# Later layers of a two-block transformer: the input product of the GELU layer in fp16 parts, four norms of a steady iteration on another engine, and a new order of stages around them

## The reference, cut to what matters

```python
x2 = _layernorm(x, g1, be1)
q = x2 @ wq.T ; k = x2 @ wk.T ; v = x2 @ wv.T        # elu + 1 on q and k
x = x + linear_attention(q, k, v)
x2 = _layernorm(x, g2, be2)                          # this is y below
h = gelu(x2 @ w1.T + b1, approximate=False)          # w1: 1024 x 256
x = x + (h @ w2.T + b2)
```

## Time and profile before

| | |
|---|---|
| median of 3 runs | 3226.55 us (3226.42 to 3232.63) |
| the profiled execution | 3230.64 us |
| its span in the trace | 3228.8 us |
| mean granted TensorE clock | 0.979 |
| PE busy | 2933.4 us, 91% |
| ACT busy | 2332.3 us, 72% |
| DVE busy | 1480.0 us, 46% |
| POOL busy | 214.9 us, 7% |

### The profile page before, as it was taken

How to read it: one execution, slowest core, us unless ns; L and a number is a source line. 1 busy time by engine, 2 the same in 40 slices (tenths; PEclk the granted TensorE clock), 3 DMA queues, 4 the chain that set the end, 5 groups by cost and what they waited for, 6 DMA issues and landing times. The chain is left out here.

```text
span 3228.8 us, 48001 instructions
## 1 busy us (share of the span) xinstructions
PE 2933.4 (91%) x18048; PEld 1173.8 (36%) x18048; DVE 1480.0 (46%) x3536; ACT 2332.3 (72%) x2586; POOL 214.9 (7%) x193
## 2 busy tenths in 40 slices
PE   2998998999999999999999998389999999999986
PEld 0221221222222222222222222256666666666654
DVE  6221220322441333232321311568888888866574
ACT  2999999999999999999999998224343334433332
POOL 0000000000000000000000000111111111111110
PEclk9999999999999999999999999699999999999998
DMA  3411111310210221111211110222122111111010
GB/s 115 141 40 36 61 37 35 102 37 33 91 39 30 88 62 42 63 35 54 71 42 35 38 41 24 64 71 60 53 71 73 59 58 58 46 53 53 26 46 21
DMA packets 125602, 177.70 MB, mean 55 GB/s; under 512 B 42248, under 2 KB 100616, under 8 KB 125128
## 3 DMA queue, kind: packets, MB, share of 16 engines
q1 hardware_dynamic: 122392, 172.53, 16.6%
q10 hardware_dynamic: 2992, 2.23, 0.2%
HBM read 107.62 MB, written 67.11 MB: 54 GB/s over the span
## 5 line engine op out<-in xcount | busy, mean ns | idle before, releaser
L717 ACT ACTIVATE probs<-ps 128x1024 f32<-128x1024 f32 x2048 | 1894.6, 1174 | 88.1 <-PE ps L456 84.6
L585 PE MATMUL ps<-probs,vals 128*32 128x512 f32 x8192 | 1096.2, 608 | 0.0
L456 PE MATMUL ps<-qT,kT 64*128 64x512 f16 x4096 | 730.4, 387 | 109.0 <-DMA kT<-split_dram 27.0
L456 PEld LDWEIGHTS ps<-qT,kT 64*128 64x128 f16 x4096 | 173.3, 93 | 1151.7 <-ACT probs L717 1026.0
L872 DVE COPY sums<-ps 128x512 f32<-128x512 f32 x64 | 44.3, 692 | 503.2 <-PE ps L585 503.2
L585 PEld LDWEIGHTS ps<-probs,vals 128*32 128x32 f32 x8192 | 162.2, 108 | 295.8 <-issue 232.9
L1307 PE MATMUL layers_ps<-yT,weight_mem 128*128 128x512 f32 x512 | 227.5, 595 | 10.9 <-ACT hT L1546 10.9
L1313 PE MATMUL layers_ps<-weight_mem,hT 128*128 128x256 f32 x1024 | 231.5, 380 | 0.0
L1573 ACT ACTIVATE gate<-layers_ps 128x512 f32<-128x512 f32 x96 | 57.3, 597 | 225.3 <-PE layers_ps L1461 225.2
L1313 PEld LDWEIGHTS layers_ps<-weight_mem,hT 128*128 128x128 f32 x1024 | 193.0, 190 | 29.8
L1461 PE MATMUL layers_ps<-n4T,weight_mem 128*128 128x512 f16 x768 | 177.2, 385 | 7.3 <-DVE n4T L1796 7.3
(11 more groups left out here) (224 smaller groups left out, 2671.8 us busy)
## 6 DMA issues: line engine op xcount, KB each, us to landing
split_dram<-parts SPq DMA_DIRECT2D x28, 768.0 KB, 3.7
qT<-split_dram SPq DMA_DIRECT2D x126, 128.0 KB
kT<-split_dram SPq DMA_DIRECT2D x126, 128.0 KB
heads_dram<-result SPq DMA_DIRECT2D x64, 128.0 KB, 7.4
...
```

Source lines behind the costliest of these rows:

```text
L456: last = nc.tensor.matmul(SCORES[slot][:, n * BANK:(n + 1) * BANK], kT[buf][rows, j * P:(j + 1) * P], qT[buf][rows, q0:q0 + BANK], start=T ...
L585: mm = nc.tensor.matmul(ACC[32 * c:32 * c + 32, :], vals[buf][:, j, :], probs[:, j % PROBS, c * BANK:(c + 1) * BANK], start=(j == 0), stop ...
L717: nc.scalar.activation(probs[:, j % PROBS, half * T // 2:(half + 1) * T // 2], SCORES[slot_of(at)], ACT.Exp, scale=OPERAND_SCALE ** -2).th ...
```

## The change

The weights `w1` are split once, in the first part, into two fp16 numbers each (high and low), in place. For that DVE finds the largest magnitude of `w1` (the reduction over partitions on POOL now has two columns), nine small instructions make the scales, and three instructions over 2048 columns make the parts. `y` is split in the same way: ACT writes its high part from PSUM, a new DVE stage `y_low` the low part. `fc0` and `fc1` then take three fp16 products (high x high, low x high, high x low) instead of one fp32 product, and the GELU takes the scale back.

Iterations 4 to 11 get orders of their own (`"full"`). In them ACT applies four norms (`ap_attn`, `ap_n1`, `ap_f`, `ap_n2`: `rstd * x + shift`) that DVE applied before. For six norms DVE also makes the negated mean and POOL, behind the power, its product with `rstd` (`shift`), in every iteration. In `full` the stage `o` stands behind `k_feat` and `y_low`, `b2` behind `in0`, and on PE `down3` ahead of `q`. In the order `all` of iterations 1 to 3 and 12, 13 `y_low` stands behind `k_feat`, in `drain` behind `o`.

```diff
+                if last_group and e == 3:
+                    parts_of_w1()
...
+            def parts_of_w1():
+                ch = Chain(dve, weights_ready, W1_SCALED)
+                scaled, w1 = flat(xs[:, 0:KC * F1 // C, :]), flat(W["w1"])
+                high, low = (w1.bitcast(FP16)[:, s * KC * F1:(s + 1) * KC * F1] for s in range(2))
+                ch.link(V.tensor_scalar(scaled, w1, fc_scale[:, 1:2], None, ALU.mult))
+                ch.link(V.tensor_copy(high, scaled))
+                ch.link(V.tensor_tensor(low, scaled, high, ALU.subtract))
...
+    if {"0", "1", "2", "b"} <= set(streams):
+        return "full"
...
+                    if l in shifted:
+                        pool.wait_ge(sem("rstd_" + l), 2 * c + 1)
+                        pool.tensor_tensor(shift[l][:, :], neg_mean[l][:, :], rstd[l][:, :], ALU.mult).then_inc(sem("rstd_" + l), 1)
...
-                        chan_out(ps[:, 6 + i % 2, :], W["w1"], i, yT).then_inc(sem("fc_mm"), 1)
+                        for n, (s, t) in enumerate(((0, 0), (1, 0), (0, 1))):
+                            for k in range(KC):
+                                last = nc.tensor.matmul(ps[:, 6 + i % 2, :], w1_16[:, s, k, i * P:(i + 1) * P], yT16[:, t, k, :],
+                                                        start=(n == k == 0), stop=(n == 2 and k == KC - 1))
+                        last.then_inc(sem("fc_mm"), 1)
...
-                A(yT[:, :, :], banks(0, 2), ACT.Copy).then_inc(sem("yT_done"), 1)
+                A(yT16[:, 0, :, :], banks(0, 2), ACT.Copy, scale=y_scale).then_inc(sem("yT_high"), 1)
...
+            def norm_apply(l, dst, src, c):
+                act.wait_ge(sem("rstd_" + l), 2 * c + 2)
+                for k in range(K4):
+                    ins = A(dst(k), src(k), ACT.Identity, scale=rstd[l][:, k:k + 1], bias=shift[l][:, k:k + 1])
+                return ins
...
+                if l in shifted:
+                    dve.wait_ge(sem("rstd_" + l), 2 * c)
+                    V.tensor_scalar(neg_mean[l][:, :], mv[l][:, :, 0], -1.0, None, ALU.mult)
...
+            def y_low(c, past):
+                dve.wait_ge(sem("yT_high"), c + 1)
+                V.scalar_tensor_tensor(yT16[:, 1, :, :].rearrange("p a n -> p (a n)"), wide(0, 2), y_scale, yT16[:, 0, :, :].rearrange("p a n -> p (a n)"),
+                                       ALU.mult, ALU.subtract).then_inc(sem("yT_done"), 1)
```

More of the change, by code:

```diff
@@ L1094, in _ @@
             second_half(NHD - 1, False)
-            dve.wait_ge(weights_ready, 3)
+            dve.wait_ge(weights_ready, W1_SCALED + 3)
 SHIFT = {"0": -EARLY, "1": 1 - EARLY, "2": 2 - EARLY, "l": LEAD, "m": LEAD + 1, "a": LEAD + 2, "b": LEAD + 3, "c": LEAD + 4}
 FIRST_CHUNK = {stream: EARLY if stream in "012" else 0 for stream in SHIFT}
-STAGES = {"0": "load_in in0 in1 in2 keep_x1", "1": "mix mix_r mix_k val f x2 n2 u", "2": "uT k k_low k_feat v q q_low q_feat kv", "l": "load_msg diag", "m": "msg y yT",
+STAGES = {"0": "load_in in0 ap_attn in1 in1_add in2 ap_n1 keep_x1", "1": "mix mix_r mix_k val f ap_f x2 x2_add n2 n2_eps ap_n2 u", "2": "uT k k_low k_feat v q q_low q_feat kv", "l": "load_msg diag", "m": "msg y yT y_low",
           "a": "load_x2 b2 fc0 fc1 proj0 proj1 proj2 proj3 o",
-          "b": "x4 n4 nT n4_low keep up0 up1 up2 up3 up4 up5 high0 high1 high2 high3 high4 high5 low0 low1 low2 low3 low4 low5 down0 down1 down2 down3",
-          "c": "ffn out"}
+          "b": "ap_o x4 x4_add n4 nT n4_low keep up0 up1 up2 up3 up4 up5 high0 high1 high2 high3 high4 high5 low0 low1 low2 low3 low4 low5 down0 down1 down2 down3",
+          "c": "ffn ap_ffn out out_add"}
 STREAM = {stage: stream for stream, stages in STAGES.items() for stage in stages.split()}
@@ L1115 @@
     "all": "fc0 mix fc1 uT mix_k mix_r nT val up0 up1 proj0 up2 up3 proj1 msg proj2 up4 up5 proj3 v k down0 yT down1 down2 q kv down3".split(),
+    "full": "fc0 mix fc1 uT mix_k mix_r nT val up0 up1 proj0 up2 up3 proj1 msg proj2 up4 up5 proj3 v k down0 yT down1 down2 down3 q kv".split(),
     "drain": "fc0 fc1 nT proj0 up0 up1 proj1 up2 up3 proj2 msg proj3 up4 up5 down0 yT down1 down2 down3".split()}
@@ L1119 @@
     "all": "fc0 mix fc1 uT mix_k mix_r nT keep up0 up1 high0 high1 up2 up3 high2 high3 up4 up5 high4 high5 v k yT q keep_x1".split(),
+    "full": "fc0 mix fc1 uT mix_k mix_r nT keep up0 up1 high0 high1 ap_f up2 up3 high2 high3 ap_n2 up4 up5 high4 high5 ap_attn v k yT q keep_x1 ap_n1".split(),
     "drain": "fc0 fc1 keep nT up0 up1 high0 high1 up2 up3 high2 high3 up4 up5 high4 high5 yT".split()}
@@ L1122 @@
     "fill": "mix k_low in0 k_feat q_low in1 q_feat f in2 x2 kv n2 u".split(),
-    "all": "ffn x4 b2 mix out n4 in0 n4_low f up0 up1 low0 low1 x2 up2 up3 low2 low3 msg n2 up4 up5 low4 low5 u y k_low o k_feat in1 q_low in2 q_feat kv diag".split(),
-    "drain": "x4 b2 ffn n4 out n4_low up0 up1 low0 low1 up2 up3 low2 low3 msg up4 up5 low4 low5 y o diag".split()}
+    "all": "ffn x4 b2 mix out n4 in0 n4_low f up0 up1 low0 low1 x2 up2 up3 low2 low3 msg n2 up4 up5 low4 low5 u y k_low o k_feat y_low in1 q_low in2 q_feat kv diag".split(),
+    "full": "ffn x4 mix out n4 in0 b2 n4_low f up0 up1 low0 low1 x2_add up2 up3 low2 low3 msg n2_eps up4 up5 low4 low5 u y k_low k_feat y_low o in1_add q_low q_feat kv diag".split(),
+    "drain": "x4 b2 ffn n4 out n4_low up0 up1 low0 low1 up2 up3 low2 low3 msg up4 up5 low4 low5 y o y_low diag".split()}
 SP_ORDER = dict.fromkeys(PE_ORDER, "load_in load_msg load_x2 x2 n2 q_feat out".split())
 UNCOUNTED = [(name, count) for count, names in (
-    (1, "mix_mm k_mm val_mm uT_mm k2_mm v2_mm q_mm kv_mm n1T_done k_read x1_kept attn_normed x1_done carried f_done x2_step u_step kv_done"),
+    (1, "mix_mm k_mm val_mm uT_mm k2_mm v2_mm q_mm kv_mm n1T_done k_read x1_kept attn_normed x1_done carried f_done x2_step u_step kv_done rstd_attn rstd_x1 rstd_f rstd_x2"),
     (2, "stats_attn stats_x1 stats_f stats_x2 n2_step"),
@@ L1584, in program @@
             def program(exact16):
-                stages = {"mix": mix, "mix_r": mix_r, "mix_k": mix_k, "uT": turn_u, "v": attn_v, "k": k_exp, "q": q_exp, "keep_x1": keep_x1, "keep": keep_x4, "yT": turn_y,
+                stages = {"mix": mix, "mix_r": mix_r, "mix_k": mix_k, "uT": turn_u, "v": attn_v, "k": k_exp, "q": q_exp, "keep_x1": keep_x1, "ap_attn": apply_attn, "ap_n1": apply_n1, "ap_f": apply_f, "ap_n2": apply_n2, "ap_o": apply_o, "ap_ffn": apply_ffn, "keep": keep_x4, "yT": turn_y,
                           "fc0": fc(0), "fc1": fc(1), "nT": turn_n4(exact16), **{f"up{m}": up(m, exact16) for m in range(M2)}}
```

88 lines of the change are left out of this document (73 added, 15 removed).

## The result

| | before | after |
|---|---|---|
| median of 8 runs each, same chip | 3226.91 us (3226.29 to 3238.92) | 3238.72 us (3236.08 to 3242.09) |
| the profiled execution, its span | 3230.64, 3228.8 | 3238.64, 3236.8 |
| mean granted TensorE clock | 0.979 | 0.967 |
| PE busy | 2933.4 us | 2900.1 us |

A forecast was written before the change was run, and what follows sets the result against it. PE bounds the kernel, with DVE's chain to `mix_k` setting each iteration's end. Filling -1.5, loop -4.9, clock -3.4, iterations 12 to 14 +4.7, drain -4.2 and +1.7 give -7.6; forecast 3220 us, range 3205 to 3232.

The forecast's parts named there:

- PE's work: `fc` matmuls on PE: 13.7 us a chunk becomes 10.35, 3.4 us less, 54 us over 16 chunks if PE alone decided.
- DVE's chain in the loop: DVE from `k_low` to `mix_k` in full iterations: 0.7 to 0.9 us shorter, 0.7 taken as each iteration's gain.
- Whether the GELU path overtakes: Third `fc` block in `fc0`: GELU late but not last, `n1T` at 2503.0 before DVE comes to `mix` at 2504.4.
- PE work with 1.4 us of slack: PE behind the GELU wait in `fc0`: low clock costs 0 to 0.7 us an iteration, taken as nothing.
- The wait of 4.8 us: PE at the third `fc` block in `fc0`: waits 4.8 us for the GELU, often making the clock fall.
- The slower rival: GELU chain at the third `fc` block becomes the bound: iteration 0.9 us longer, +8 in all, 3235; chance 0.17.
- The two clock falls at `mix_k`: `xk` records in two of seven iterations: low clock after PE's wait goes, two times 1.69 us, -3.4 in the sum.
- Filling: Iterations 2 to 4: late `q` against 3.4 us less `fc`, -1.5 us taken, between -3 and +2.
- Iterations 12 to 14: Order `all`, `q` waits for `y_low`: +1.3, +0.8 and +2.6 us, sum +4.7.
- Drain: Iterations 15 to 18: `keep` waits for the output addition, gain 1.05 us each, 4.2 in all; clock falls cost +1.7.

The follow-up runs named there:

- b2_moved: The kernel before with one edit, `b2` behind `in0` instead of ahead of `mix` in the order `all`: ratio to before 0.9926, median 3211.8 us.
- warm: The changed kernel plus five extra fp32 matmuls, never read, behind the second `fc` block in full iterations: ratio to before 0.9985, median 3229.9 us.
- all_fixed: The changed kernel with order `all` mended: `k_feat` and `y_low` ahead of `o`, `down3` ahead of `q`: ratio to before 1.0003, median 3234.4 us.
- norms_only: The changed kernel with `fc` in fp32, no `y_low`, `w1` not split, new orders and ACT norms kept: ratio to before 1.0025, median 3243.0 us.
- tuned_fp32: The best reordered version of the changed kernel, with `fc` in fp32, no `y_low`, `w1` not split: ratio to before 0.9955, median 3217.0 us.

## Why the prediction was wrong

*PE's work.* Right: 3.4 us less a chunk where the clock is up (12 matmuls in 2.75).

*DVE's chain in the loop.* Right, to 0.1 us. From `k_low` to `q_low` 11.6 us (2483.78 to 2495.37), as worked out. With DVE's last statistic at 2508.04 and 4.6 us of mixing, `xr` would be ready at 2512.7; with its hand-over of 0.2 `mix_k` would start 29.1 after `k_low` where it was 29.9 before. That is the 0.7 to 0.9 forecast. The `xk` pair takes 1.41 as in the earlier trace rows, and `b2` in its new place leaves `n4_low` at 1.23 us. b2_moved shows the same for the kernel before.

The Trainium skill ("GPSIMD Engine Reference", "Specifications") has contention where both inputs are in SBUF; that `n4_low`, with one input in PSUM, goes free beside `b2` follows from it, and the trace agrees (1.23 us).

*Whether the GELU path overtakes.* This is the step that failed. Its parts: the norm on ScalarE took 2.06 us and not 1.5, and two GELUs 1.45 and not 1.26, since the scale is now an operand. That is 0.6 (the prediction's own two rows give 1.7 us for the norm when they are solved for a column and an instruction, not 1.5), and the third block came 19.0 us after `k_low` began, where 18.4 was forecast. The error is the sentence "what it slows is PE work with 1.4 us of slack: 0 to 0.7 us an iteration, taken as nothing". Two blocks at half clock take 2.3 us more (5.02 against 2.75), and they stand on the path to `n1T`, so `n1T` comes 1.6 us after DVE is free for it. The wait of 4.8 us was forecast, that the clock would fall often was forecast, and the price was taken from 1.69 us, the extra of eight `xk` records after a wait of 2 us. After a wait of 5 us the whole stretch of 12 matmuls is slow.

That the slow restart is paid after each idle gap is what the Trainium skill says ("TensorE: Matmul & The Clock Gate", section "HAM oscillation — how this bites in real kernels"); the prediction cited it and then gave it no price in the sum. It holds in all eight iterations that stand behind a full one (4.98 to 5.30 us for these 12 matmuls), and warm shows what it costs.

Result for the loop: 75.11 us in an iteration where an undisturbed one of before takes 74.41, so +0.7 where -0.7 was forecast. The slower rival had this place, this mechanism and +0.9, but with 2.8 us for the norm. That its total, +8 and 3235, is what the span shows is luck: the terms it lists add up to +9.4 (+7.9 with the filling's -1.5), its loop was +7.2 where -0.3 was measured, and the filling and iterations 12 to 14 lost what the loop did not. The two clock falls at `mix_k` did go.

*Filling.* Forecast -1.5, measured +5.3 by iteration 4, of which 1.5 lie ahead of the first `mix_k`. I took the 3.4 us of `fc` as a gain there, and the late `q`, named in this term too, as less than it. The new place of `y_low` in all_fixed takes back only 1.3. The most of the rest, 2.3 us by iteration 3, stays in all_fixed and is 0.2 in norms_only and tuned_fp32, counted in the same way: these have no `y_low`, so it comes with the fp16 parts in any order tried here.

*Iterations 12 to 14.* Forecast +4.7, measured +8.1 from 12 to 15. The mechanism is right: `q` waits for `y_low`, which ends at 2867.24 in iteration 12 (PE's time line),

```profile
2867.45 3.67 PE L1352 MATMUL layers_ps<-uT,weight_mem 128*128 128x512 f32 x8 [2.37 <-issue]
```

and it costs 2.6 us there by all_fixed. (`up0` of iteration 13 waits 2.38 us and runs at the low clock, but it did so before the change.) The other 2.5 of iteration 12's 5.1 are the GELU path again: its `fc0` waits for a GELU behind the `ap_n1` of iteration 11,

```profile
2803.18 4.98 PE L1484 MATMUL layers_ps<-yT,weight_mem 128*128 128x512 f16 x12 [5.17 <-ACT hT L1595]
```

so `mix_k` starts 20.7 us after the first `fc` matmul where it was 18.2. That a boundary iteration inherits the last full one's chain was not in my working.

*Drain.* Forecast -4.2 and +1.7. `keep` behind the output addition was the right reading, and the wait of 2.1 us was as forecast. The clock fell behind it in iterations 14 and 15. Iteration 15 loses 2.8, 16 to 20 gain 7.9. In sum -5.1 against -2.5.

By its terms, measured with forecast in brackets: up to iteration 4 +5.3 (-1.5), iterations 4 to 11 -0.3 (-8.3), 12 to 14 +8.1 (+4.7), from 15 -5.1 (-2.5): +8.0 (-7.6).
